# A GRU scan behind a depthwise convolution: the first x on ScalarE's queue, W_hh's last part in two transfers, n of step 0 in its own bank, products for zero matmuls

## The reference, cut to what matters

```
x = x + causal_depthwise_conv(x, w = cond_2048[:, None, :])     # 16 taps, 512 channels
x = x + GRU(initial_state = cond_2048, inputs = x)

def cell(h, x):                     # one step of 256, batch 16, D = 512
    gi = x @ W_ih + b_ih            # [16, 1536]: r, z, n
    gh = h @ W_hh + b_hh
    r = sigmoid(i_r + h_r)
    z = sigmoid(i_z + h_z)
    n = tanh(i_n + r * h_n)
    return (1 - z) * n + z * h
```

## Time and profile before

| | |
|---|---|
| median of 3 runs | 1030.17 us (1030.14 to 1030.59) |
| the profiled execution | 1029.93 us |
| its span in the profile | 1028.2 us |
| TensorE matmul busy | 1016.2 us (99%) |
| VectorE busy | 865.4 us (84%) |
| ScalarE, GpSimd busy | 401.3 us (39%), 238.7 us (23%) |

### The profile page before, as it was taken

How to read it: one execution, slowest core, us unless ns; L and a number is a source line. 1 busy time by engine, 2 the same in 40 slices (tenths; PEclk the granted TensorE clock), 3 DMA queues, 4 the chain that set the end, 5 groups by cost and what they waited for, 6 DMA issues and landing times.

```text
span 1028.2 us, 58208 instructions
## 1 busy us (share of the span) xinstructions
PE 1016.2 (99%) x24836; PEld 915.7 (89%) x24836; DVE 865.4 (84%) x2850; ACT 401.3 (39%) x1816; POOL 238.7 (23%) x784
## 2 busy tenths in 40 slices
PE   8999999999999999999999999999999999999997
PEld 5987777777888888899999999999999999999995
DVE  6778888888888888888888898888888877777554
ACT  4333433334343343434334333343433433334342
POOL 3212222222222222222222222222222222222222
PEclk9999999999999999999999999999999999999999
DMA  7721001010000101001010010101001010000000
GB/s 289 75 38 39 18 15 35 11 39 18 28 24 13 35 18 34 21 13 35 15 39 19 15 35 11 39 19 29 25 11 35 14 29 18 10 29 4 25 14 12
DMA packets 66450, 32.07 MB, mean 31 GB/s; under 512 B 43920, under 2 KB 65040, under 8 KB 66192
## 3 DMA queue, kind: packets, MB, share of 16 engines
q1 hardware_dynamic: 65760, 28.25, 10.7%
q10 hardware_dynamic: 432, 0.11, 0.1%
HBM read 19.86 MB, written 8.49 MB: 28 GB/s over the span
## 4 chain that ended last, share of the span: by engine, by line
PE 94%; issue 2%; SPq 2%; POOL 1%; DMA 1%; DVE 0%; ACT 0%; POOLq 0%; DVEq 0%
PE pg L308 63%; PE pg L298 31%; SPq L185 1%; POOL tz L260 1%; DMA xw<-x 0%; SPq L179 0%; DMA cnd<-cond 0%; DVE hp L543 0%; PE pcv L336 0%; POOL nzh L273 0%; DVE gn L522 0%; DVE gt L518 0%; ACT rz L440 0%; POOLq L44 0%; POOL cpad L250 0%
## 5 line engine op out<-in xcount | busy, mean ns | idle before, releaser
L308 PE MATMUL pg<-whh,hp 128*32 128x192 f32 x16368 | 718.0, 326 | 4.9 <-DVE hp L543 2.8
L308 PEld LDWEIGHTS pg<-whh,hp 128*32 128x32 f32 x16368 | 603.8, 110 | 68.5 <-issue 2.7
L298 PE MATMUL pg<-wih,x 128*32 128x192 f32 x8192 | 386.0, 326 | 0.0
L273 POOL TENSOR_TENSOR nzh<-rz,hp 128x32 f32<-128x32 f32 x512 | 159.1, 311 | 783.1 <-ACT rz L440 783.1
L298 PEld LDWEIGHTS pg<-wih,x 128*32 128x32 f32 x8192 | 301.4, 110 | 30.6
L440 ACT ACTIVATE rz<-gt 128x64 f32<-128x64 f32 x512 | 136.2, 266 | 486.7 <-DVE gt L518 463.7
L485 DVE SCALAR_TENSOR_TENSOR x<-xb,cnd,x 128x512 f32<-128x512 f32 (+1 forms) x420 | 294.9, 702 | 7.9
L543 DVE TENSOR_TENSOR_SCAN hp<-zcp,nzh 128x96 f32<-128x96 f32 x512 | 173.7, 339 | 42.1 <-ACT nzh L445 41.4
L518 DVE STREAM_TRANSPOSE gt<-pg 128x128 f32<-128x128 f32 x512 | 160.5, 313 | 53.5 <-PE pg L308 45.0
L530 DVE TENSOR_TENSOR_SCAN an<-rz,gn 128x64 f32<-128x64 f32 x512 | 149.4, 292 | 52.1 <-ACT rz L440 51.6
L445 ACT ACTIVATE nzh<-an 128x32 f32<-128x32 f32 x512 | 122.1, 238 | 125.6 <-DVE an L530 125.6
(11 more groups left out here) (45 smaller groups left out, 45.6 us busy)
## 6 DMA issues: line engine op xcount, KB each, us to landing
xb<-x SPq DMA_DIRECT2D x96, 94.0 KB, 2.0
out<-x SPq DMA_DIRECT2D x60, 128.0 KB, 1.9
wih<-w_ih SPq DMA_DIRECT2D x4, 768.0 KB, 7.8
whh<-w_hh SPq DMA_DIRECT2D x4, 768.0 KB, 14.3
xw<-x SPq DMA_DIRECT2D x24, 64.0 KB, 3.4
xb<-x SPq DMA_DIRECT2D x16, 62.0 KB, 1.9
tz<-taps SPq DMA_DIRECT2D x12, 64.0 KB, 3.2
xs<-x SPq DMA_DIRECT2D x1, 512.0 KB, 4.7
```

Of the source, the lines that this page charges most:

```text
L273: pool.tensor_tensor(nzh[:, f, ::2, :, 1], chunks(rz[:, f, 1, :, 1]), h_of(t - 1, slice(f * CH, (f + 1) * CH)), ALU.mult).then_inc(s_zh[f], 1)
L298: i = pe.matmul(pg[m % Q][f][D * j:D * (j + 1), RZ:END], x1_of(c, 2 * m, 2 * m + 2), wih[:, c, :, :].rearrange("p (g k) (j d) -> p j g k d ...
L308: i = pe.matmul(pg[t // 2 % Q][f][D * j:D * (j + 1), 0:IN], hp[:, t % 2, 2 * c + 1 - t % 2:2 * c + 3 - t % 2, :, 1].rearrange("p u b -> p ...
```

## The change

1. `xs` is issued by ScalarE's queue as its first DMA, ahead of the two biases. SyncE issues `cnd` and then W_ih at once.
2. The last column of W_hh comes in two transfers: r and z (512 KB, `s_whh[3]`), then n (256 KB, `s_whl`). SyncE waits for `whh[2]` only before it issues `xb`.
3. h's share of n for step 0 goes to the bank `pcv[1]`, opened by a thirteenth zero matmul, seeded by two more ScalarE copies, and read from there by `transpose_n(0, f)` behind `s_gn`. r and z of column 3 are signalled ahead of n. TensorE no longer waits for `s_whn` in step 0.
4. After c = 0 stands product(2, 0, 3) and three zero matmuls, after c = 1 product(2, 1, 3) and four; after c = 2 product(2, 0, 0); behind step 0 only the products (2, 0, 1) and (2, 0, 2); in step 1 three products instead of four.
5. The turns of column 3 move from step 8 to step 9, its spreads from steps 9 to 11 to steps 10 and 11.

```
-IDLE = {1: 4, 2: 2}
+IDLE = {0: 3, 1: 4}
...
-        ROUNDS = {1: 4, 2: 6, 3: 8}
-        TURNED = {1: (5, 7), 2: (7, 9), 3: (9, 12)}
+        ROUNDS = {1: 4, 2: 6, 3: 9}
+        TURNED = {1: (5, 7), 2: (7, 9), 3: (10, 12)}
...
-            sp.dma_start(xs[:, :, :], x[:, :, 0:TB * B]).then_inc(s_xs, 16)
...
-            for c in range(C):
+            for c in range(C - 1):
                 sp.dma_start(whh[:, c, F:], w_hh[:, c, :]).then_inc(s_whh[c], 16)
-            for c in range(C):
-                sp.wait_ge(s_whh[c], 16)
+            sp.dma_start(whh[:, C - 1, F:3 * F], w_hh[:, C - 1, 0:2 * F]).then_inc(s_whh[C - 1], 16)
+            sp.dma_start(whh[:, C - 1, 3 * F:], w_hh[:, C - 1, 2 * F:]).then_inc(s_whl, 16)
+            sp.wait_ge(s_whh[C - 2], 16)
...
-            def product(m, f, c):
+            def product(m, f, c, last=C - 1):
...
+                if m == 2 and c == C - 1:
+                    pe.wait_ge(s_seed[f], m + 1)
...
-                if c == C - 1:
+                if c == last:
                     i.then_inc(s_gi[f], 1)
...
+            def recur_rz(f, c):
+                for j in range(J):
+                    i = pe.matmul(pg[0][f][D * j:D * (j + 1), RZ:IN],
+                                  hp[:, 0, 2 * c + 1:2 * c + 3, :, 1].rearrange("p u b -> p (u b)"),
+                                  whh[:, c, F:3 * F].rearrange("p (g j f n) -> p j f g n", g=2, j=J, f=H)[:, j, f],
+                                  start=False, stop=True, skip_group_check=True)
+                return i
...
+            def recur_n(f, c):
+                for j in range(J):
+                    i = pe.matmul(pcv[1][D * j:D * (j + 1), f * RZ:(f + 1) * RZ],
+                                  hp[:, 0, 2 * c + 1:2 * c + 3, :, 1].rearrange("p u b -> p (u b)"),
                                   whh[:, c, 3 * F:].rearrange("p (j f n) -> p j f n", j=J, f=H)[:, j, f],
                                   start=False, stop=True, skip_group_check=True)
                 return i
...
+            pe.matmul(pcv[1][:, :], zeros[:, 0:P], zeros[:, :], start=True, stop=True).then_inc(s_bits, 1)
...
-            for c in range(C):
+            pe.wait_ge(s_seed_n, H)
+            for c in range(C - 1):
                 pe.wait_ge(s_whh[c], 16)
-                if c < C - 1:
-                    pe.wait_ge(s_whn, c + 1)
                 for f in range(H):
-                    if c < C - 1:
-                        recur(0, f, c)
-                    else:
-                        recur_first(f, c).then_inc(s_gh[f], 1)
+                    recur_rz(f, c)
+                    recur_n(f, c)
+                if c < H:
+                    product(2, c, C - 1, C - 2)
                 for _ in range(IDLE.get(c, 0)):
                     pe.matmul(pcv[0][:, :], zeros[:, 0:P], zeros[:, :], start=True, stop=True)
-            for c in range(C):
-                product(2, 0, c)
+            product(2, 0, 0, C - 2)
+            pe.wait_ge(s_whh[C - 1], 16)
+            for f in range(H):
+                recur_rz(f, C - 1).then_inc(s_gh[f], 1)
+            pe.wait_ge(s_whl, 16)
+            recur_n(0, C - 1)
+            recur_n(1, C - 1).then_inc(s_gn, 1)
+            for c in range(1, C - 1):
+                product(2, 0, c, C - 2)
...
-                    if m + 2 < M2:
-                        product(m + 2, t % 2, c)
+                    if m + 2 < M2 and not (t == 1 and c == C - 1):
+                        product(m + 2, t % 2, c, C - 2 if t == 1 else C - 1)
...
+            act.dma_start(xs[:, :, :], x[:, :, 0:TB * B]).then_inc(s_xs, 16)
             act.dma_start(bih[:, :], b_ih).then_inc(s_small, 16)
             act.dma_start(bhh[:, :], b_hh).then_inc(s_small, 16)
...
+            for f in range(H):
+                act.activation(pcv[1][:, f * RZ:(f + 1) * RZ], bc[:, f, 0:RZ], ACT.Copy).then_inc(s_seed_n, 1)
...
+                if t == 0:
+                    dve.wait_ge(s_gn, 1)
+                g = pg[t // 2 % Q][f][:, 0:RZ] if t else pcv[1][:, f * RZ:(f + 1) * RZ]
```

More of the change, by code:

```diff
@@ L90, in build @@
         s_whh = [sem(f"s_whh{c}") for c in range(C)]
+        s_whl = sem("s_whl")
         s_whn = sem("s_whn")
@@ L113, in build @@
         s_x1 = sem("s_x1")
+        s_seed_n = sem("s_seed_n")
         s_seed = halves("s_seed")
@@ L116, in build @@
         s_tin = halves("s_tin")
+        s_gn = sem("s_gn")
         s_gh = halves("s_gh")
@@ L312, in recur @@
                 return i
-            def recur_first(f, c):
-                hh = hp[:, 0, 2 * c + 1:2 * c + 3, :, 1].rearrange("p u b -> p (u b)")
+            def recur_rz(f, c):
                 for j in range(J):
[L318 to L322, removed]
+                    i = pe.matmul(pg[0][f][D * j:D * (j + 1), RZ:IN],
[7 more added lines that the diff above has]
+                                  hp[:, 0, 2 * c + 1:2 * c + 3, :, 1].rearrange("p u b -> p (u b)"),
                                   whh[:, c, 3 * F:].rearrange("p (j f n) -> p j f n", j=J, f=H)[:, j, f],
@@ L411, in seed @@
                 if m < Q:
-                    act.wait_ge(s_bits, 2 * Q)
+                    act.wait_ge(s_bits, 2 * Q + 1)
                     act.wait_ge(s_bc, H)
@@ L432, in _ @@
             for c in range(C):
-                act.wait_ge(s_whh[c], 16)
+                act.wait_ge(s_whh[c] if c < C - 1 else s_whl, 16)
                 act.activation(whh[:, c, 0:F], whh[:, c, 3 * F:], ACT.Copy).then_inc(s_whn, 1)
@@ L521, in transpose_n @@
             def transpose_n(t, f):
+                if t == 0:
+                    dve.wait_ge(s_gn, 1)
+                g = pg[t // 2 % Q][f][:, 0:RZ] if t else pcv[1][:, f * RZ:(f + 1) * RZ]
                 dve.transpose(gn[:, t // 2 % 2, :, f, :, :, 0].rearrange("p u c b -> p c u b"),
-                              pg[t // 2 % Q][f][:, 0:RZ]).then_inc(s_tn[f], 1)
+                              g).then_inc(s_tn[f], 1)
             def scan_n(t, f):
```

## The result

The changed kernel takes 1037.07 us (median of 5 runs, 1036.34 to 1037.64) against 1030.14 us for the kernel before, measured beside it: ratio 1.0069, 95% interval 1.0058 to 1.0080, so 0.7% slower. Its profiled execution has a span of 1035.2 us, 7.0 more than before. The prediction had the direction and the chain of waits, but it gave 3.0 us where 6.9 were measured, and its range ended at 1036.8.

The account below looks back on a forecast made before the run. TensorE, busy 99% of the span, was taken to bound the kernel. Queue loss 4.7 plus clock loss 1.6 minus gains 3.3 made it 3.0 us slower, 1033.2 us; the range was 1027.5 to 1036.8.

Parts of the forecast that it names:

- What bounds: TensorE is busy 99% of the span; ahead of step 0, delaying VectorE's start on x at 5.98 delays step 0.
- The gains: Step 0, step 1 and column 3's turns, TensorE at full clock: 1.9 + 0.3 + 1.1, together 3.3 us gained.
- Step 0: From its first matmul to VectorE's start on r and z: 5.3 us, 1.9 us gained.
- Step 1: One product less on TensorE: 0.3 us gained, at most 0.33, at least nothing.
- The later n: In step 0 n's matmuls end 0.5 us after r and z's: cost nothing, or 0.2 us without cover by the sigmoid.
- The turns: Column 3's turns, moved to step 9, no longer make TensorE wait for an operand: 1.1 us gained.
- The queue: ScalarE's queue at the start: biases behind x land near 9.4, VectorE starts on x at 10.7: 4.7 us lost.
- The biases' own term: Behind x on ScalarE's queue, the biases take 18 turns against W_ih at 0.25 us, 4.5 us.
- x takes turns too: At the start x also alternates with W_ih's packets: 9.4 us lost there, +7.7 in sum, 1037.9 us; chance 0.15.
- The clock: After TensorE idles four microseconds, 3.4 us of step 0 run at half speed: 1.6 us lost, bounds 0 and 2.6.
- The first rival: Biases pass right behind x on ScalarE's queue, VectorE starts 0.7 to 1.0 us late: 1027.9 us, faster; chance 0.23.

Follow-up runs that it names:

- the two kernels on them: Changed kernel with x on SyncE's queue and column 3's turns back in step 8: 1027.85 us; kernel before with only the turns moved to step 9: 1028.63 us.
- the zeros in the idle time: Changed kernel, x on ScalarE's queue, with fifteen more zero matmuls between the products and step 0: 1035.16 us, 1.0050 to the kernel before.
- the kernel without zeros: Changed kernel with x back on SyncE's queue and no zero matmuls in step 0 (IDLE empty): 1026.49 us, 0.9970 to the kernel before.

## Why the prediction was right in kind and wrong in size

**What bounds.** Right: VectorE's start on x decides once it is late, and the shift at 5.98 went through to step 0's first matmul within 0.03 us (8.48 and 8.45).

**The gains, 3.3 us.** Right. Undoing part 1 alone gave 3.3 to 3.9 us over the kernels before (1026.82 against 1030.14 and 1030.72). Step 0 was put at 5.3 us and took 5.45. Step 1 was put at 0.3 and gave 0.20. The later n was put at nothing, or 0.2 uncovered: the way from VectorE's start to step 1 grew by 0.17. The turns were put at 1.1, and the two kernels on them give 1.0 to 1.7 and 1.4. One reason in that part was wrong: SyncE's earlier start brings nothing, since its loads of `xw` wait for h; the move by a step brings it all.

**The queue, put at 4.7 us, measured 8.48.** This is the step that failed, and it is one sentence of it: "x, issued 0.45 before W_ih and all in one issue, should then pass mostly ahead and land near 5.98 - 0.45 = 5.5". It landed at 9.5, 8.7 us after its issue; with W_ih held back it took 4.3. The row for 3.5 to 6.9 us showed that the stream that is ahead has packets lined up; I gave x, which was ahead by 0.44, the same privilege for all of its 32 packets per engine. The trace after shows 144 packets of ScalarE's queue between 2 and 3 us, 9 an engine, and then both queues side by side: 333 packets against 198 from 3 to 7 us, with three quarters of the engines' time spent on W_ih's. So the 4.0 us between 5.5 and 9.5 are packets of W_ih that went between x's own. The biases' own term was right: 3.85 us from x's landing to theirs (9.5 to 13.35), where I had put 18 turns of 0.25, 4.5 us, less the 0.6 from the last packet to the landing. The rival "x takes turns too" had the mechanism and 9.4 us for it, but a chance of 0.15 only. The row weighed against it showed the taps, issued 1.9 us behind x and 1.2 behind W_ih on the other queue, where x had a head start of 0.44.

The rule of the Trainium skill ("DMA: Bandwidth & Descriptors", section "Queues, rings and completion order") that an engine goes round its queues a packet at a time is what this trace shows, 403 packets to 403. Taken as it stands, without the exception that I read into one row, it leads to the rival at 1037.9, 0.8 us above the measured time. From 3 to 7 us, with 333 packets to 198, the trace agrees with it in kind and not in the count.

**The clock, put at 1.6 us, measured 1.7.** Step 0 took 7.01 us where 5.3 was its full-clock length, and the zeros in the idle time gave back 1.6 from step 0 to step 1. Right, together with the place: the products ended at 22.07, step 0 began 4.02 us later, and the half clock lay within it. That it came so was not certain: where the clock falls differs from trace to trace, as the last section shows. With a start at 14.46 put in, the prediction's own sum is 8.5 + 1.6 - 3.3 = 6.8 us, and 6.9 were measured.

**The first rival** (the biases slip through, faster) needed them at 8.0 or earlier. It took a hold of 1.5 us on W_ih to bring that about, and then it was 0.24% faster.

## What to carry to other kernels

A second DMA queue is not a second road. While the other queue streamed packets of 6 KB, each packet of 48 bytes (403 to 403) or of 1 KB (477 to 486) let about one of them pass. Count the packets per engine of everything that is issued about when a stream begins, and multiply by the time of one turn: here the biases' 18 turns at 5.7 x 16 / 403 = 0.23 us are 4.1 us, and 3.85 were measured. Put the loads that the first work waits for ahead of the stream. x did well in the stream's own queue in front of it (4.6 and 4.7 us to landing). Then ask of each engine which of its loads it waits for first: here the 12 KB of biases, not the 512 KB of x that had been moved for its own good.

## What the runs showed that was not expected

- The second bias, 6 KB, took 2.4 us when issued at 1.25 with W_ih issued at 1.96, 3.8 behind x with W_ih held back to 2.78, 4.8 when issued at 1.24 with W_ih issued at 1.26, 6.8 when issued at 1.70 behind x's and W_ih's issues on the other queue, and 11.2 behind x in a queue that took turns with W_ih.
- x, 512 KB, landed 4.3 us after its issue with W_ih issued 1.97 us behind it, 8.7 with a head start of 0.44 us, and 14.5 when issued 0.48 us behind W_ih and behind both biases.
- The granted clock did not fall at the same place in each trace. In the changed kernel TensorE kept 1.00 through 4.0 us of idle time and lost it about 0.6 us after step 0 had begun. With x alone on ScalarE's queue it fell about 1.0 us ahead of step 0, within the idle time; with W_ih held back it fell after an idle time of only 2.06 us. In the kernel without zeros, idle times of 1.2 and 0.7 us ahead of and in step 0 did not cost it; in the kernel before, 1.17 and 0.98 us at the same places were followed by the half clock.
